# Moving row statistics, value banks and output products around the start of a batch in a two-layer transformer kernel

## What is computed

```python
xn = layernorm(x)
x = x + attn0(xn, Q, K, V, W) + ffn0(xn, router_weight, ..., shared_down_w)
# attn0: 16 heads of 64, causal softmax(q k^T) v, then projected by W and summed over heads
# ffn0: 32 experts of hidden width 64, top 6 of them weighted per row, plus one shared expert of 128
xn = layernorm(x)          # needs mean and variance of every row of the first layer's result
x = x + attn1(xn, ...) + ffn1(xn, ...)
```

## Time and profile before

| | |
|---|---|
| median of 3 runs | 1165.15 us (1164.19 to 1165.21) |
| profiled execution, its own time | 1166.57 us |
| its span, first to last instruction | 1164.8 us |
| TensorE busy | 1144.8 us (98%) |
| VectorE busy | 1000.9 us (86%) |
| ScalarE busy | 839.3 us (72%) |
| GpSimd busy | 481.9 us (41%) |
| granted TensorE clock | 1.000 |

### The profile page before, as it was taken

One profiled execution on the slowest core, in us unless ns is written; L12 is line 12 of the kernel. 1 busy time (PEld: TensorE's weight loads), 2 busy tenths in 40 slices (PEclk: granted clock), 3 DMA queues, 4 the chain that ended last, 5 costly groups with the idle time before them and its releaser, 6 DMA issues.

```text
span 1164.8 us, 24229 instructions
## 1 busy us (share of the span) xinstructions
PE 1144.8 (98%) x8988; PEld 900.1 (77%) x8988; DVE 1000.9 (86%) x1917; ACT 839.3 (72%) x2240; POOL 481.9 (41%) x423
## 2 busy tenths in 40 slices
PE   8999999999999999999999999999999999999998
PEld 7778777777777877787777777877778767777776
DVE  6989798979887989798988888898888788898897
ACT  5886777577757775777677767776777767887886
POOL 2337600760067006700670067006660477735741
PEclk9999999999999999999999999999999999999999
DMA  7014101410032004100420042004400430000000
GB/s 268 2 31 137 55 1 31 136 57 1 31 128 64 1 31 128 65 1 24 128 71 1 14 131 78 1 5 131 128 1 4 129 97 1 2 21 19 2 11 28
DMA packets 44949, 63.93 MB, mean 55 GB/s; under 512 B 8224, under 2 KB 19104, under 8 KB 44576
## 3 DMA queue, kind: packets, MB, share of 16 engines
q1 hardware_dynamic: 44832, 62.39, 16.8%
HBM read 59.48 MB, written 2.88 MB: 54 GB/s over the span
## 4 chain that ended last, share of the span: by engine, by line
PE 78%; DVE 13%; issue 4%; ACT 3%; DMA 1%; SPq 0%; POOL 0%; DVEq 0%; ACTq 0%; POOLq 0%
PE psum L1714 14%; PE psum L1733 13%; PE psum L1655 11%; PE psum L65 9%; PE psum L67 8%; PE psum L66 8%; PE psum L1668 3%; DVE probs L1353 2%; PE psum L1680 2%; DVE sg L1343 2%; DVE sg L1353 2%; PE psum L1987 2%; PE psum L1737 1%; DVE probs L1343 1%; DMA crow<-weights 1%
## 5 line engine op out<-in xcount | busy, mean ns | idle before, releaser
L829 ACT ACTIVATE probs<-psum,mneg 128x256 f32<-128x256 f32 (+3 forms) x400 | 187.1, 485 | 109.1 <-DVE mneg L1278 109.1
L1714 PE MATMUL psum<-ident,probs 128*128 128x128 f32 x1600 | 210.1, 276 | 3.8 <-ACT probs L871 3.5
L1278 DVE TENSOR_REDUCE mneg<-psum 128x2 f32<-128x1024 f32 (+3 forms) x256 | 194.7, 819 | 20.5 <-PE psum L1668 16.6
L1269 DVE COPY pt<-psum 128x512 f32<-128x512 f32 x256 | 165.0, 684 | 46.2 <-PE psum L1714 44.4
L1714 PEld LDWEIGHTS psum<-ident,probs 128*128 128x128 f32 x1600 | 178.0, 141 | 28.4 <-ACT probs L829 8.2
L573 POOL TENSOR_TENSOR rstd<-var,mhalf 128x4 f32<-128x4 f32 x7 | 7.1, 1012 | 337.0 <-DVE var L1162 337.0
L1733 PE MATMUL psum<-pt,v_all 128*64 128x384 f32 (+5 forms) x1088 | 142.6, 412 | 0.0
L1733 PEld LDWEIGHTS psum<-pt,v_all 128*64 128x64 f32 (+1 forms) x1088 | 69.7, 135 | 62.7 <-issue 50.2
L65 PE MATMUL psum<-xt_hi,gu_hi 128*128 128x512 f32 x272 | 110.2, 405 | 0.0
L67 PE MATMUL psum<-xt_hi,gu_lo 128*128 128x512 f32 x272 | 107.9, 397 | 0.0
L66 PE MATMUL psum<-xt_lo,gu_hi 128*128 128x512 f32 x272 | 107.3, 394 | 0.0
(11 more groups left out here) (306 smaller groups left out, 2912.8 us busy)
## 6 DMA issues: line engine op xcount, KB each, us to landing
crow<-weights SPq DMA_DIRECT2D x256, 128.0 KB, 3.0
rrow<-sums SPq DMA_DIRECT2D x128, 128.0 KB, 3.0
gu_raw<-in_gu SPq DMA_DIRECT2D x1, 2176.0 KB, 13.0
x_all<-in_x SPq DMA_DIRECT2D x8, 256.0 KB, 5.3
out_rows<-x_all SPq DMA_DIRECT2D x7, 256.0 KB, 2.3
down_raw<-in_down SPq DMA_DIRECT2D x1, 1088.0 KB, 13.0
wqkv_raw<-in_wqkv SPq DMA_DIRECT2D x1, 768.0 KB, 6.4
wqkv_raw<-in_wqkv SPq DMA_DIRECT2D x1, 512.0 KB, 5.3
```

Source lines behind the costliest of these rows:

```text
L829: last = act.activation(probs[:, h * HALF + PROB[t]:h * HALF + PROB[t] + w], bank[score_bank(rnd, c) + h][:, o:o + w], ACT.Exp, bias=mneg[ ...
L1269: dve.tensor_copy(pt[:, s % 2, :, 3 - s // 2, :], turn_bank(rnd, s).rearrange("p (j q) -> p j q", q=P)).then_inc(pt_ready, 1)
L1278: last = dve.tensor_reduce(mneg_h[:, :, t], psum[:, b:b + 2, o:o + P * (t + 1)], AX, ALU.max, negate=True)
L1714: last = nc.tensor.transpose(dst[:, i * P:(i + 1) * P], probs[:, v:v + P], ident[:, :])
```

## The change

It has three parts. (1) `row_stats` is cut in two: for batches 1 to 6 `bn_stats` of batch b-1 runs in slot 7 behind the variances of b+1, and the rest (`sum_row_stats`) at unit 0 behind the last copy of probabilities; unit 14 no longer has it. (2) The values of batches 1 to 7 go over banks 6, 4, 5; fill f waits for fill f-3 to be copied, fills 1 and 2 for the q and k of pair 0, fill 0 for nothing. (3) In the head, `unit_down(b-1, 14)` goes ahead of the first scores, and all four `project_out` of batch b-1 stand at the end of `first_head`, ahead of slot 0's score group; `acc_done` is raised there. ScalarE's and GpSimd's lists are as before.

```diff
--- before.py
+++ after.py
@@ -267,11 +267,12 @@
                 return bank[4], bank[5]
             return bank[6], bank[7]
 
+        VALUE_BANKS = [6, 4, 5]
         VALUE_BANK_FIRST = [2, 3, 4, 5, 4, 7, 4, 7]
 
         def value_bank(b, f):
 
-            return bank[4 + f % 2] if b else bank[VALUE_BANK_FIRST[f]]
+            return bank[VALUE_BANKS[f % 3]] if b else bank[VALUE_BANK_FIRST[f]]
 
         def logits_bank(b):
 
@@ -444,7 +445,7 @@
 
 
 
-        NORM_AFTER, STATS1_AFTER, ROWS_AFTER, LOGITS_AFTER, QK_AFTER, V_AFTER = 1, 14, 5, 7, 9, 12
+        NORM_AFTER, ROWS_AFTER, LOGITS_AFTER, QK_AFTER, V_AFTER = 1, 5, 7, 9, 12
 
         ROWS1_AFTER, TURN1_AFTER = [5, 7, 9], [8, 10, 12]
 
@@ -1252,6 +1253,8 @@
                     stats0(b + 1)
                 if p == 7 and b < B - 1:
                     variances0(b + 1)
+                    if b:
+                        add_row_stats(b - 1, x_all[:, b - 1, :, :])
 
             def rest_q(n, scale):
                 dve.wait_ge(qk_hi_ready, n * 2 + 1)
@@ -1391,6 +1394,8 @@
                 for u in range(UNITS):
                     if u == 0:
                         take_turned(n, [3])
+                        if 0 < b < B - 1:
+                            sum_row_stats(b - 1, x1_var_ready)
                     gate(b * UNITS + u, u)
                     if b < B - 1 and u == QK_AFTER + 1:
                         rest_q((b + 1) * PAIRS, SCALE0)
@@ -1402,8 +1407,6 @@
                     if b < B - 1:
                         if u == NORM_AFTER:
                             norm_rows(b + 1, xn)
-                    if 0 < b < B - 1 and u == STATS1_AFTER:
-                        row_stats(b - 1, x_all[:, b - 1, :, :], x1_var_ready)
                     if b < B - 1:
                         if u == ROWS_AFTER:
                             split_xt(b + 1)
@@ -1413,11 +1416,17 @@
                         add_lora()
                 low_part(b * UNITS + UNITS - 1, UNITS - 1)
 
-            def row_stats(b, src, out_sem):
-                s = slice(b * TILES, (b + 1) * TILES)
+            def add_row_stats(b, src):
                 for t in range(TILES):
                     last = dve.bn_stats(stats[:, b * TILES + t, :], src[:, t, :])
                 chain.step(last)
+
+            def row_stats(b, src, out_sem):
+                add_row_stats(b, src)
+                sum_row_stats(b, out_sem)
+
+            def sum_row_stats(b, out_sem):
+                s = slice(b * TILES, (b + 1) * TILES)
                 for t in range(TILES):
                     last = dve.bn_aggr(mv[:, b * TILES + t, :], stats[:, b * TILES + t, :])
                 chain.step(last)
@@ -1634,10 +1643,10 @@
                             pe.wait_ge(logits_taken, 1)
                         if f in (4, 6, 7):
                             pe.wait_ge(v_taken, f - 1)
-                    elif f >= 2:
-                        pe.wait_ge(v_taken, b * FILLS + f - 1)
-                    else:
-                        pe.wait_ge(qk_lo_ready, b * PAIRS * 2 + f + 1)
+                    elif f >= 3:
+                        pe.wait_ge(v_taken, b * FILLS + f - 2)
+                    elif f:
+                        pe.wait_ge(qk_lo_ready, b * PAIRS * 2 + f)
                     c, n = slice(t * P, (t + 1) * P), PAIRS // VHALVES
                     w = [v[:, 2, half * n:(half + 1) * n, :].rearrange("p n m -> p (n m)") for v in (wqkv_hi, wqkv_lo)]
                     split_matmul(nc, value_bank(b, f), (xt_hi[:, b % 2, c], xt_lo[:, b % 2, c]), w, True, True).then_inc(v_done, 1)
@@ -1867,9 +1876,6 @@
                     pe.wait_ge(combt_ready, b + 1)
                 if p:
                     weigh_pair(n - 1)
-                elif b:
-                    project_out(b - 1, 2)
-                    project_out(b - 1, 3).then_inc(acc_done, 1)
                 if p == PAIRS - 1:
                     if b:
                         pe.wait_ge(x1_ready, b)
@@ -1900,17 +1906,18 @@
                 pe.wait_ge(v_taken, (b + 1) * FILLS)
                 project_qk(n + 1, [0])
                 project_qk(n + 1, [1])
+                unit_down(b - 1, UNITS - 3)
                 pe.wait_ge(qk_lo_ready, n * 2 + 2)
                 pe.wait_ge(su_done, b * UNITS)
                 score_masks(n, 0, True)
                 score_products(n, 0, True).then_inc(scored, 1)
-                unit_down(b - 1, UNITS - 3)
                 score_masks(n, 1, True)
                 score_products(n, 1, True).then_inc(scored, 1)
                 unit_down(b - 1, UNITS - 2)
                 unit_down(b - 1, UNITS - 1)
-                project_out(b - 1, 0)
-                project_out(b - 1, 1)
+                for i in range(PAIRS // 2):
+                    last = project_out(b - 1, i)
+                last.then_inc(acc_done, 1)
 
             def units(b):
                 n = (b + 1) * PAIRS - 1
```

## The result

The changed kernel takes 1174.01 us (median of 5 runs, 1173.64 to 1175.6) against 1165.21 us of the kernel before in the same comparison: a ratio of 1.0077 (95% interval 1.0065 to 1.0088), 8.8 us slower. The forecast was 1172.8 us. The profiled execution took 1173.67 us with a span of 1171.9 us, 7.1 us above that of before. One of the executions of the kernel before that stand beside e5 to e8 took 1582.88 us at a granted clock of 0.655; it is left out of the ratios, since in all others the clock was 0.999 or 1.000.

What follows compares the result with a forecast made beforehand. It took TensorE, busy 98% of the span, plus its waits as the bound. Head 1 +2.0, six other heads 1.26 each, value banks -1.9 gave +7.7 us on 1165.15: 1172.8 us, range 1169 to 1177.5 (1164 to 1178 with B and D).

Steps and rivals of the forecast that it cites:

- The hole and the statistics: Heads 2 to 7, TensorE ahead of the first masks: moving the statistics closes a 0.84 us hole, at no cost elsewhere.
- Rival D: Slot 7 and unit 0: the moved statistics are not covered, at most 5.2 us more, 1175.4 to 1178.0 us; chance 0.10.
- The value banks: Value fills: with three banks, four TensorE waits for ScalarE's copy of an earlier fill go, 1.9 us gained (0 to 2.0).
- The first wait: Each head, last output product: TensorE waits 1.1 us for GpSimd's low parts, which end at T0 + 9.55.
- T0: In each head, the time at which TensorE could start the work behind q/k of pair 1.
- the sum: Whole kernel: +2.0 in head 1, 6 x 1.26 in the others, 1.9 gained at value fills, together +7.7 us.
- Rival B: Heads: GpSimd's low parts are in time, so only the accumulator-copy wait stays: -0.7 us, 1164.4 us; chance 0.09.
- The second wait: Each head, q of pair 2: TensorE waits 1.0 us for ScalarE's accumulator copy, which stands behind the third chunk's exponentials.
- P - T0: Length of a head from T0 to q of pair 2: forecast 14.92 us, against 12.91 (head 1) and 13.66 (others) before.
- Rival C: Heads: neither the wait for low parts nor that for the accumulator copy binds: -7.8 us, 1157.3 us; chance 0.08.
- Rival E: Heads: two 1 us holes 5 us apart drop TensorE's clock to 1.2 GHz, 90 us more, 1263 us; chance 0.02.

Runs made afterwards that it cites:

- e5: The changed kernel with ScalarE's copy of the accumulator moved ahead of the third chunk's exponentials: 1171.9 us, 1.0054 of the kernel before.
- e8: The kernel before with only unit 14's down product moved ahead of the first masks: 1162.9 us, 0.9979 of the kernel before.
- e1: The kernel before with only the statistics moved out of unit 14, into slot 7 and unit 0: 1160.69 us, 0.9958 of before.
- e7: The changed kernel with the accumulator copy ahead of the third chunk's exponentials and low parts of pairs 6 and 7 on VectorE: 1164.11 us, 0.9986 of before.
- parts 1 and 2 alone: The kernel before with the statistics moved and the values over three banks, the head unchanged: 1159.4 us, 0.9946 of before.
- e3: The kernel before with only the head changed (unit 14 down first, all four output products ahead of the score group): 1180.05 us, 1.0122.

## Why the prediction was right

**The hole and the statistics.** Right, shown by e1. In the changed kernel both pieces lie under cover, as the timeline of VectorE in slot 7 and unit 0 of batch 1 shows; it answers to the earlier trace rows:

```profile
198.60 0.87 DVE L1421 BATCH_NORM_STATS2 stats<-x_all 128x6 f32<-128x128 f32 x4
199.76 0.69 DVE L1272 COPY pt<-psum 128x512 f32<-128x512 f32 x1 [0.29 <-PE psum L1723]
...
203.43 0.17 DVE L1433 TENSOR_SCALAR nmean<-mv 128x4 f32<-128x4 f32 x1
...
203.97 0.69 DVE L1346 TENSOR_TENSOR sg<-sg,psum 128x512 f32<-128x512 f32 x1 [0.30 <-ACT sg L921]
```

0.29 and 0.30 us are left, where I had reckoned 0.14 and 0.08, since instructions on VectorE overlap at their ends (`bn_stats` starts 0.09 us before the end of the row ahead of it). `nmean` takes 0.17 in its new place, beside an idle GpSimd, in all six batches; in the kernel before it took 1.19 to 1.21 in all six, started 0.12 us behind an operation of GpSimd and ended within 0.03 us of it. Rival D falls. This trace agrees with the Trainium skill ("SBUF — State Buffer", section "Who interferes with whom"), by which the two engines block each other only where both need the shared ports: `nmean` fell from 1.21 us beside GpSimd's work to 0.17.

**The value banks.** 1.9 us forecast, 1.8 measured between the heads of the changed kernel, where part 1 shares in it; 1.4 alone.

**The first wait.** The position of GpSimd's end was right to 0.01 us (T0 + 9.55 against 9.54). Its size was forecast at 1.1 and is 0.98, since the product's turn comes at T0 + 8.61 and not 8.5. Two errors of mine partly cancel there: the changes between scores and products are worth 0.30 us (e8) and not 0.15, which brings the turn forward, and the third output product's own wait of 0.20, which I had not seen, puts it back. All that does not enter the sum, as the end of the wait and not its start sets what follows. Rival B falls: freeing VectorE at unit 14 brought heads 2 to 7 to head 1's picture (14.89 to 15.02).

**The second wait.** 1.0 forecast, 1.06 measured, and P - T0 = 14.92 forecast, 14.91 measured. Rival C falls in two ways: both waits bind, and in e7, which has neither, the kernel is 1.2 us under the kernel before and not the 7.8 us of C, and 4.7 us slower than parts 1 and 2 alone.

**The clock.** Rival E falls: the granted clock was 1.0 in all five executions of the changed kernel.

**What I had not seen.** First, 0.45 us once, in slot 1 of batch 7: k of pair 3 starts 1.22 us behind q (863.99) instead of 0.79. There GpSimd prepares the second layer, and two operations of the router on VectorE (`rl`, `corr`) run beside it, ahead of the copy that k waits for. VectorE, GpSimd and TensorE in the changed kernel:

```profile
862.73 0.82 DVE L1214 TENSOR_TENSOR rl<-rexp,route_sum 128x128 f32<-128x128 f32 x1
863.58 0.85 DVE L1215 TENSOR_TENSOR corr<-rl,ebias 128x128 f32<-128x128 f32 x1
```

```profile
861.76 1.64 POOL L657 TENSOR_TENSOR rrow<-rrow,bias_bf 32x768 f32<-32x768 f32 x1
863.47 0.82 POOL L658 CAST bias_bf<-rrow 32x768 bf16<-32x768 f32 x1
```

```profile
865.21 0.50 PE L65 MATMUL psum<-xt_hi,wqkv_hi 128*128 128x512 f32 x1 [0.27 <-DVE pt L1272]
```

In the kernel before, `corr` took 0.85 us there as well, but `rl` 0.39: it started when GpSimd's operation had 0.24 us left, and here 0.67. In batch 3 of e5 both take 0.29. So the loss depends on where in GpSimd's list the slot happens to fall, and not on the slot being later: in e8, whose slot comes earlier than in the kernel before (`rl` at 852.70 against 856.16), `rl` took 0.83. Second, and larger for what it teaches: I wrote that the products behind the score group cover the copy of the accumulator. They cover a whole chain, and the copy is only its first link. Rival C priced the kernel without the two waits at 1157.3 us; e7 stands at 1164.1. The sum did not need this, since the named waits were the longer ones. No run has the order of the change with neither wait and nothing else moved, so how much of the 6.8 us between C and e7 belongs to the edits of e7 itself is not shown; 5.2 us of it are k and slot 1.

Two slips in the prediction's figures change nothing: by its own terms the lower end of its range is 1169.9 us, not 1169, and the chances of faster, same and slower leave out E's 0.02, which belongs to slower.

The medians differ by 8.8 us where the sum had 7.7: 0.45 of the rest is the collision in batch 7, and the rest is within the interval (7.6 to 10.3 us).

## What to carry to other kernels

Work that stands behind a short group of matmuls may look as if it could go anywhere, since it waits for nothing and TensorE is busy either way; if the group feeds a chain through other engines, that work is what TensorE does while the chain runs. Before moving such work forward, add up the chain from the group's start to the first matmul that needs its end, and compare it with what is left behind the group. And when a wait is taken away, price the next one in the same chain: here a copy moved for 7 us gave 2.

## What the runs showed of the hardware

A change between matmuls of 64 rows (scores) and of 128 rows (products) costs some 0.15 us: `unit_down` 14 put ahead of both score chunks makes two of them fewer and saved 0.30 us in a head without any wait (12.91 to 12.61, head 1 of e8). What in such a change takes the time is not shown. A wait of TensorE that the profile shows as 0.81 us idle costs 0.98 to 1.06 us against the matmul's turn. Two such waits 5 us apart, seven times over, left the granted clock at 1.00. A VectorE instruction on 128x4 numbers (`nmean`) takes 0.17 us, also when it starts 0.14 us ahead of a GpSimd multiplication (e3, batch 6), but 1.19 to 1.21 us when it starts 0.12 us behind one (the kernel before, six times): it then ends with GpSimd's operation.
